# Moving small pieces of work in a fused adaLN, attention and expert-routing kernel

## The reference

```
mod = silu(c) @ wmod            # 4 x 6 x 512: sa, ca, ga, sb, cb, gb
ga, gb = sign(.) * max(abs(.), 0.25)
h = layernorm(x) * (1 + ca) + sa
q, k, v = h @ Wq + bq, h @ Wk + bk, h @ Wv + bv     # 16 heads of 128
a = softmax(q @ k.T / sqrt(128) + causal mask) @ v
x = x + ga * (a @ Wo + bo)
h = layernorm(x) * (1 + cb) + sb
w, idx = top2(softmax(h @ gate.T))                   # of 8 experts; w normalised to sum 1
y = sum over the 2 experts of w * (silu(h @ Wg.T) * (h @ Wu.T)) @ Wd.T
y = y + the same with the shared expert's weights    # 704 wide, no routing weight
return x + gb * y
```

## Time and profile before

| | |
|---|---|
| median of 3 runs (lowest to highest) | 1568.44 us (1567.68 to 1570.82) |
| the profiled execution / its span | 1572.1 us / 1569.9 us |
| mean granted TensorE clock | 0.989 of full speed |
| TensorE busy | 1520.4 us, 97% |
| VectorE busy | 1006.4 us, 64% |
| ScalarE busy | 731.9 us, 47% |
| GpSimd busy | 713.6 us, 45% |
| moved by DMA | 304.03 MB, mean 194 GB/s |

### The profile page before, as it was taken

How to read it: one execution, slowest core, us unless ns; L and a number is a source line. 1 busy time by engine, 2 the same in 40 slices (tenths; PEclk the granted TensorE clock), 3 DMA queues, 4 the chain that set the end, 5 groups by cost and what they waited for, 6 DMA issues and landing times.

```text
span 1569.9 us, 29503 instructions
## 1 busy us (share of the span) xinstructions
PE 1520.4 (97%) x8844; PEld 1355.2 (86%) x8844; DVE 1006.4 (64%) x2224; ACT 731.9 (47%) x1738; POOL 713.6 (45%) x761
## 2 busy tenths in 40 slices
PE   6899999998999999999999999998999999999998
PEld 3677778887999999999999999988989899999986
DVE  5876676667777777777777777795467322222268
ACT  2542222345666666666666666653331233333333
POOL 2103333346656566656565666667813211111055
PEclk9999999999999999999999999999999999999999
DMA  7334555568757666666757484653333456756455
GB/s 259 134 121 171 199 189 196 204 238 295 236 166 239 188 202 185 213 198 190 214 165 238 147 246 143 224 208 135 123 124 141 168 195 213 285 200 236 147 181 188
DMA packets 203292, 304.03 MB, mean 194 GB/s; under 512 B 80384, under 2 KB 142208, under 8 KB 196048
## 3 DMA queue, kind: packets, MB, share of 16 engines
q1 hardware_dynamic: 196096, 281.80, 53.1%
q0 software_dynamic: 5680, 18.62, 3.9%
q10 hardware_dynamic: 1440, 2.62, 0.5%
HBM read 187.35 MB, written 115.64 MB: 193 GB/s over the span
## 4 chain that ended last, share of the span: by engine, by line
PE 86%; DVE 6%; ACT 2%; issue 2%; DMA 2%; POOL 2%; another core or an unknown queue 0%; POOLq 0%; SPq 0%; ACTq 0%; DVEq 0%
PE bank L1553 45%; PE bank L1648 17%; PE bank L1763 8%; PE bank L1715 7%; PE bank L1746 4%; PE bank L1813 2%; PE bank L1566 1%; PE bank L1849 1%; DMA xin<-ffn_rows 1%; POOL h L1226 1%; ACT prob L1373 1%; DVE h_lo L2027 0%; POOL acc L1218 0%; ACT h_raw L1248 0%; DVE row_max L2200 0%
## 5 line engine op out<-in xcount | busy, mean ns | idle before, releaser
L1553 PE MATMUL bank<-w,xt_hi 128*128 (+2 forms) x1136 | 286.7, 334 | 10.8 <-DVE xt_lo L2176 7.8
L1553 PEld LDWEIGHTS bank<-w,xt_hi 128*128 128x128 f32 x1136 | 200.8, 192 | 17.8 <-issue 8.5
L1553 PE MATMUL bank<-w,xt_lo 128*128 (+2 forms) x568 | 186.1, 328 | 0.0
L1385 ACT ACTIVATE prob<-prob,row_inv 128x128 f32<-128x128 f32 (+3 forms) x256 | 137.2, 560 | 81.9 <-DVE row_inv L2213 81.9
L2349 DVE TENSOR_TENSOR ht_lo<-bank,ht_hi 128x128 fp32r<-128x128 f32 (+1 forms) x213 | 48.4, 282 | 185.0 <-ACT ht_hi L1493 181.2
L1373 ACT ACTIVATE prob<-bank,neg_max 128x128 f32<-128x128 f32 (+3 forms) x256 | 133.6, 525 | 44.0 <-DVE neg_max L2205 44.0
L1553 PE MATMUL bank<-wv_hi,h_hi 128*128 128x256 f32 x512 | 147.0, 287 | 0.0
L1553 PE MATMUL bank<-w,ht_hi 128*128 (+3 forms) x426 | 139.2, 408 | 6.5 <-DVE ht_lo L2349 5.7
L1553 PE MATMUL bank<-wv_hi,h_lo 128*128 128x256 f32 x512 | 144.7, 283 | 0.0
L1553 PE MATMUL bank<-wv_lo,h_hi 128*128 128x256 f32 x512 | 144.7, 283 | 0.0
L2200 DVE TENSOR_REDUCE row_max<-bank 128x1 f32<-128x128 f32 (+3 forms) x256 | 119.8, 489 | 6.6
(11 more groups left out here) (245 smaller groups left out, 4151.6 us busy)
## 6 DMA issues: line engine op xcount, KB each, us to landing
keys<-k_ring SPq DMA_DIRECT2D x64, 512.0 KB, 3.0
ch_raw<-wexp SPq DMA_DIRECT2D x128, 170.0 KB, 3.1
experts_hi<-ch_hi SPq DMA_DIRECT2D x128, 170.0 KB, 2.6
experts_lo<-ch_lo SPq DMA_DIRECT2D x128, 170.0 KB, 2.7
w<-experts_hi SPq DMA_DIRECT2D x10, 2176.0 KB, 7.9
w<-experts_lo SPq DMA_DIRECT2D x10, 2176.0 KB, 14.6
q_transposed<-q_out SPq DMA_DIRECT2D x64, 256.0 KB, 2.0
k_even<-keys SPq DMA_DIRECT2D x16, 1024.0 KB, 5.8
```

Of the source, the lines that this page charges most:

```text
L1385: ins = act.activation(part, part, ACT.Copy, scale=row_inv[:, h, r:r + 1])
L1553: ins = pe.matmul(dst, a, m, start=(k == 0), stop=(k == last))
```

## The change

1. **Modulation pieces.** Piece 1 goes to bank 0, so it no longer waits for the copy of piece 0. Pieces 3 and 2 are made right after the transposes of the first batch, into banks 6 and 7. Their weights go to a new buffer, `mod_early`, which lies where `t_parts0` lies later; SyncE issues their loads before the second batch's activations and no longer waits for the transposes. ScalarE copies piece 2 aside to `mod_raw`, and VectorE clamps it where it did. TensorE no longer makes piece 3 after plain(0) nor piece 2 after half 4.
2. **First attention step.** ScalarE and VectorE split the first group of values at the step's start, and the first transposed part before the last two normalisations.
3. **Norm rows of the first batch.** All four tiles are ScalarE's (one pass) and GpSimd's (two), in the last step. VectorE's `c_rows` is gone. GpSimd's passes stand between its residual passes for the second and third batch. The second batch's statistics are taken before the last additions to `acc` for two tiles and after the first split of stage 3 for the others; the split gate weights (`gate_columns`) come earlier.
4. **Slot tables.** Their three parts run one job sooner, the first two right after the gate product, and the third before the pass that adds up the shared result.
5. **Loops.** ScalarE's and VectorE's routed jobs are written out, 39 jobs, in place of the loop of two.

The two engines' order in the first attention step is in the diff. Cut to its core:

```diff
+        mod_early = sbuf(s1m, "mod_early", [P, 2, DC, D])
+        mod_raw = sbuf(s1, "mod_raw", [B, D])[:, :]
...
             sp.dma_start(stage[2], wq_v[:, :, 0:D]).then_inc(wq0_ld, 16)
+            mod_weights(3, mod_early[:, 0])
+            mod_weights(2, mod_early[:, 1])
             sp.dma_start(xs[1], x_t[:, TT:2 * TT, :]).then_inc(x_ld[0], 16)
             sp.wait_ge(mod_full, 1)
             raw_weights(0)
-            sp.wait_ge(tx_full, TT)
-            mod_weights(3, w_x)
...
-                if tail >= 0:
-                    loaded(tail)
-                    c_pre(tail)
-                if last:
+                if tail == 0:
+                    loaded(0)
+                    c_pre(0)
+                if tail == 1:
+                    loaded(1)
+                    c_pre(1, [0])
+                    c_rows(0, 0)
+                    c_pre(1, range(1, TT))
+                if tail == 2:
+                    c_rows(0, 1)
+                    loaded(2)
+                    c_pre(2, [0])
+                    c_rows(0, 2)
+                    c_rows(0, 3)
+                    c_pre(2, [1])
                     c_seed_of(1)
+                    c_pre(2, range(2, TT))
...
-                        act.wait_ge(mod_full, 3)
+                        act.wait_ge(mod_full, 4)
+                        act.activation(mod_raw, bank[7][0:B, :], ACT.Copy)
...
                 if first:
+                    v_part(0)
...
                     normalise(3, n)
-                    v_part(0)
                     exps(5, n)
+                    pt_part(0, 0)
                     normalise(4, n)
                     normalise(5, n)
-                    for g in range(3):
-                        pt_part(0, g)
+                    pt_part(0, 1)
+                    pt_part(0, 2)
...
                     v_part(0)
+                    if last:
+                        c_rows(0, 0)
...
                     normalise(5, n)
+                    if last:
+                        c_rows(0, 1)
...
+                else:
+                    c_rows(0, 2)
+                    c_rows(0, 3)
...
-            with act.Fori(R0 // 2 + 1, Z0 // 2 - 1) as j:
-                for k in range(2):
-                    job(j * 2 + k, k, "routed", True)
+            for n in range(R0 + 2, Z0 - 3):
+                job(n, n % 2, "routed", True)
...
-            mod_piece(1, stage[1], 6)
+            mod_piece(1, stage[1], 0)
...
             for i in range(1, TT):
                 transposes(0, i)
+            mod_piece(3, mod_early[:, 0], 6)
+            mod_piece(2, mod_early[:, 1], 7)
...
-                if b == 0:
-                    mod_piece(3, w_x, 6)
...
-                if norm2:
-                    c_rstd(0)
-                    c_rows(0, 0)
-                if norm3:
-                    gate_columns()
-                    c_rows(0, 2)
-                    c_rows(0, 3)
...
+            c_stats(1, 0)
+            c_stats(1, 1)
             for i in range(TT):
                 add_out(NIT - 1, B - 1, i)
-                c_stats(1, i)
+            xt_part(1, 1)
+            c_stats(1, 2)
+            c_stats(1, 3)
             c_moments(1)
-            xt_part(1, 1)
...
-                begun()
+                table()
...
-            shared_job(NT + 3, lambda: one_hots(1))
-            shared_job(NT + 4, tokens)
-            halves()
-            shared_job(NT + 5, table)
+            shared_job(NT + 3, lambda: one_hots(1), begun)
+            shared_job(NT + 4, tokens, halves)
+            shared_job(NT + 5)
...
-            with dve.Fori(R0 // 2 + 1, Z0 // 2) as j:
-                for k in range(2):
-                    job(j * 2 + k, k, "routed", True)
-            job(Z0 - 1, 0, "routed", True)
+            for n in range(R0 + 2, Z0):
+                job(n, n % 2, "routed", True)
```

More of the change, by code:

```diff
@@ L282, in adaln_layer @@
         s1 = ExitStack()
+        s1m = ExitStack()
+        mod_early = sbuf(s1m, "mod_early", [P, 2, DC, D])
+        s1m.close()
         t_both = [sbuf(s1, "t_parts0", [P, 12, T], F32R)]
@@ L426, in adaln_layer @@
         c_ld = sem("c_ld")
-        modw_ld = [sem("modw_ld0"), sem("modw_ld1"), sem("modw_ld_later")]
+        modw_ld = {0: sem("modw_ld0"), 1: sem("modw_ld1"), 3: sem("modw_ld_later"), 2: sem("modw_ld2")}
+        modw_ld[4] = modw_ld[5] = modw_ld[3]
         wq0_ld = sem("wq0_ld")
@@ L509, in adaln_layer @@
         c_seed = sem("c_seed")
-        c_xn = sem("c_xn")
         c_scaled = sem("c_scaled_rows")
@@ L619, in mod_weights @@
             def mod_weights(m, to):
-                sp.dma_start(to, wmod_v[:, :, m * D:(m + 1) * D]).then_inc(modw_ld[min(MOD_ORDER.index(m), 2)], 16)
+                sp.dma_start(to, wmod_v[:, :, m * D:(m + 1) * D]).then_inc(modw_ld[m], 16)
             def raw_weights(i):
@@ L1026, in c_rows @@
             def c_rows(b, t):
-                row, n = h2[:, t, :], (b - 1) * TT + t + 1
+                row, n = h2[:, t, :], b * TT + t + 1
                 pool.wait_ge(c_xa, n)
@@ L1035, in c_seed_of @@
                 pool.wait_ge(c_var, b + 1)
-                if b > 1:
-                    pool.wait_ge(c_xa, (b - 1) * TT)
+                if b:
+                    pool.wait_ge(c_xa, b * TT)
                 pool.tensor_tensor(rs0[:, :], ve[:, :], mh[:, :], ALU.pow).then_inc(c_seed, 1)
@@ L1237, in _ @@
                 act.wait_ge(mod_full, m + 1)
-                act.activation(mod_row[m], bank[6][0:B, :], ACT.Copy).then_inc(mod_ev, 1)
+                act.activation(mod_row[m], bank[(6, 0)[m]][0:B, :], ACT.Copy).then_inc(mod_ev, 1)
             def hidden(b, i):
@@ L1459, in c_rows @@
                 act.wait_ge(c_seed, (b + 1) * C_SEED)
-                act.wait_ge(h2_st, h2_stored(b - 1))
+                if b:
+                    act.wait_ge(h2_st, h2_stored(b - 1))
                 act.activation(h2[:, t, :], acc[:, b * TT + t, :], ACT.Identity, scale=rstd[:, t:t + 1],
@@ L1557, in _ @@
             pe.wait_ge(silu_c, 1)
+            MOD_FREE = {3: (mod_ev, 1), 2: (modc_ok, 2), 4: (mod_ev, 4), 5: (mod_ev, 5)}
             def mod_piece(m, w, to):
-                k = MOD_ORDER.index(m)
-                pe.wait_ge(modw_ld[min(k, 2)], 16 * max(k - 1, 1))
-                if k:
-                    pe.wait_ge(mod_ev, k)
+                pe.wait_ge(modw_ld[m], {4: 32, 5: 48}.get(m, 16))
+                if m in MOD_FREE:
+                    pe.wait_ge(*MOD_FREE[m])
                 for c in range(DC):
@@ L1624, in half @@
                                     [(q_ev, 11), (q_ev, 12), None, None, (q_ev, 13), (q_ev, 14), (q_ev, 15), (q_ev, 16)][m])
-                if v - 1 in MOD_AFTER:
+                if v - 1 in MOD_AFTER and MOD_AFTER[v - 1] != 2:
                     free[5] = (mod_ev, MOD_ORDER.index(MOD_AFTER[v - 1]) + 1)
@@ L1673, in half @@
                 product(6, plain_w(2, 1), t_rows(4))
-                if v in MOD_AFTER:
+                if v in MOD_AFTER and MOD_AFTER[v] != 2:
                     pe.wait_ge(*reader(v, 4))
@@ L2146, in half @@
                 if v in MOD_AFTER:
-                    mod_piece(MOD_AFTER[v], bank[half_banks(v + 1)[5]][0:B, :])
+                    m = MOD_AFTER[v]
+                    mod_piece(m, mod_raw if m == 2 else bank[half_banks(v + 1)[5]][0:B, :])
                 if v == 0:
@@ L2234, in step @@
                 norm2 = isinstance(p, int) and p == HP - 1 and b == 2
-                norm3 = isinstance(p, int) and p == HP - 1 and b == 3
                 if first:
+                    v_part(0)
                     maxima(0, n)
@@ L2288, in step @@
                     maxima(1, n + 1)
+                else:
+                    gate_columns()
                 o_part(1)
@@ L2320, in c_moments @@
                 dve.tensor_scalar(ve[:, :], mv[:, :, 1], EPS, None, ALU.add).then_inc(c_var, 1)
-            def c_rstd(b):
-                dve.wait_ge(c_seed, b * C_SEED + C_SEED)
-            def c_rows(b, t):
-                dve.scalar_tensor_tensor(out=h2[:, t, :], in0=acc[:, b * TT + t, :], scalar=mv[:, t, 0:1],
-                                         in1=mods[:, b, 2, :], op0=ALU.subtract, op1=ALU.mult).then_inc(c_xn, 1)
-                dve.wait_ge(c_xn, b * TT + (t + 1))
-                dve.scalar_tensor_tensor(out=h2[:, t, :], in0=h2[:, t, :], scalar=rstd[:, t:t + 1],
-                                         in1=mods[:, b, 1, :], op0=ALU.mult, op1=ALU.add).then_inc(h2_ok, 1)
             def gate_columns():
@@ L2362, in y_part, with job @@
                                   gb_row(b), ALU.mult).then_inc(y_gb, 1)
-            def job(n, s, prev, nxt, b_prev=None, after_xt=None):
+            def job(n, s, prev, nxt, b_prev=None, after_xt=None, after_mid=None):
                 if prev:
@@ L2371, in job @@
                 dve.tensor_tensor(h_mid[:, s, :], gate_s[:, s, :], bank[1][:, 0:F], ALU.mult).then_inc(mid_ok, 1)
+                if after_mid:
+                    after_mid()
                 if nxt:
```

(5 more changed lines are left out.)

4 lines of the change are left out of this document (removed).

## The result

| | before | changed |
|---|---|---|
| median (lowest to highest) | 1569.63 us (1567.68 to 1574.15), 4 runs | 1554.82 us (1553.15 to 1556.46), 4 runs |
| ratio, 95% interval | | 0.9899 (0.9876 to 0.9921) |
| span of the profiled execution | 1569.9 us | 1553.5 us |
| mean granted clock | 0.989 | 0.993 |

A forecast was written before the change was run, and what follows sets the result against it. TensorE, busy 97% of the span, was taken as the bound. Terms 1.75 + 3.60 + 0.4 + 4.15 + 4.1 + 5.0 = 19.0 us took the median from 1568.44 to 1549.4 us; 8-in-10 range 1544.5 to 1556.5 us.

The forecast's parts named there:

- First pause, +1.75 us: Before the first query products: pieces 3 and 2 keep TensorE working, saving 2.65 us, less 0.9 us at the second batch.
- The upper bound of 2.65 us: Top of the 0.95 to 2.65 us range for the net gain from filling the pause before the first query products.
- The give-back at the second batch: Without piece 3, idle there grows from 0.58 to about 4.2 us and the clock probably falls: 0.3 to 1.7, taken 0.9.
- Piece 2, +3.6 us: This modulation product leaves the stretch where TensorE never rests, saving 3.60 us.
- First attention step, +0.4 us: Splitting values 0 and 1 ahead of the score chain ends the second group of transposes about 0.4 us sooner (0 to 1.3).
- Norm rows, +4.15 us: Last attention steps to second shared job: VectorE freed, last weights then release TensorE; 3.35 us of wait plus 0.8 of clock.
- the wait's term: Before the second shared job: TensorE released by the last weights at 1061.5 us, not at 1064.85 us, gaining 3.35 us.
- the third rival: The clock survives the shortened waits at second batch (0.9 us), weights (1.7 us) and attention (1 us): 1545.8 us, chance 0.08.
- Slot tables, +4.1 us: First routed job: earlier tables remove 3.02 us of wait and 1.6 us of clock, less 0.5 us for TensorE's table read.
- Written-out loops, +5.0 us: Near the end: straight code cures two late "remote" instructions; TensorE gains 3.01 + 3.0 us, the end 5.0 (3.5 to 6).
- the first rival: Late instructions near the end are not the loops' doing but fall into GpSimd's first eight gathers and stay: 1554.4 us, chance 0.22.
- a range of its own: The forecast's span from its terms' ends, 1545.5 to 1553.5 us, carrying chance 0.53.

The follow-up runs named there:

- the second profile: Profile of the changed kernel run once more, without edits, on another chip than the four runs before it: 1550.42 us, ratio 0.9902 to the kernel before.
- the break: Changed kernel with GpSimd waiting after four of its first eight gathers until ScalarE has weighted two tiles: 1556.85 us, ratio 0.9929 to the kernel before.
- the best kernel: Changed kernel with a shorter wait amid the first eight gathers, all final additions on VectorE, modulation piece 3 after plain(0): 1546.41 us, ratio 0.9882 to before.
- the gathers spaced: Changed kernel with GpSimd waiting after its first four gathers until ScalarE has weighted two tiles: 1556.85 us, ratio 0.9929 to the kernel before.
- the tables back: Changed kernel with the slot tables' three parts at their old places: 1557.74 us, ratio 0.9937 to the kernel before.

## Why the prediction was right, and where not

- **First pause, +1.75 us.** Measured from the table: 2.4 and 2.5 us (3.36 - 0.92 and 3.30 - 0.77), 0.7 above the sum. The upper bound of 2.65 us does not follow from the terms: with 0.3 us given back at least it is 2.35, and the result lies just above that. The clock's 2.65 us came as 2.6 in every run with the change. The query products started 0.6 us sooner than the first piece's lead explains, where the sum had 0.05. The give-back at the second batch, 0.9 us, came as 0.74 and 0.66 us by 89.00 in the changed kernel and as 0.0 to 0.9 in its variants. The idle of 4.2 us there was 4.10, with the low clock behind it in every run. What the sum did not see: with one piece in the pause the query products run at full speed too, and the other piece behind plain(0) then gives 0.9 to 1.0 us.
- **Piece 2, +3.6 us.** 3.6 us in each run.
- **First attention step, +0.4 us.** 0.54 to 0.89, and 0.0 with the order undone. The sum has no term for the clock here. The two profiles with 0.9 us have a mean clock of 0.83 in the 10 us from the long wait's end, and a third with 0.54 has 0.67.
- **Norm rows, +4.15 us.** 3.6 and 3.7 us in the changed kernel. The last third of the weights released TensorE, as forecast. On the old axis (8.0 us later, the lead at 386.59) it landed at 1062.4 us against my 1061.5, the store ahead of it was issued at 1046.1 against 1045.8. So the wait's term was too large: 2.35 us in the first profile (lead 8.00 to 10.35), where the sum had 3.35. The clock's was too small in that profile: 2.2 us (10.35 to 12.59 six us further on) for 0.8. A tile's late load took 1.0 back. In the second profile it was 3.1 and 0.7. So the third rival, that the clock survives the shorter waits, came true at this place in two profiles of eleven and at the second batch in none.
- **Slot tables, +4.1 us.** 4.9 to 5.1. GpSimd's memset was no later than TensorE at all; I had kept back 0.5 us for a read that cost nothing, and 2 us come on top of the wait of 3.02 us, not 1.6.
- **Written-out loops, +5.0 us: failed.** The step "I take them for code that is not there yet, and straight code as the cure" is wrong. Straight code left both rows where they were. The words that I set against it (a stall stands at the branch, these stand jobs behind the loops' ends) were right, and the first rival, with 1554.4 us, was the outcome (1554.82). The DMA part of the trace says so too. Between 1482 and 1489 us, while both engines were late, no instruction queue moved anything; the last reads of these queues before lie between 1470 and 1482 us (the second block), and the second profile, without lateness, has the same two there:

```profile
q0 software_dynamic: 443, 1.43, 74.2%
q10 hardware_dynamic: 2, 0.00, 0.1%
```

```profile
q8 instruction: 1, 0.02, 0.5%
q14 instruction: 1, 0.01, 0.2%
```

The sum of what the second profile shows, 2.5 + 3.6 + 0.9 + 3.7 + 4.9 + 0 = 15.6 us, is near the ratio's 15.9.

So the measured time is right by the width of the range and by the first rival in it. The forecast itself had a range of its own, 1545.5 to 1553.5 us, and missed it: 5.0 us of its 19.0 were wrong in kind. That the miss is only 5.4 us has some luck in it. The other five terms came out 1.6 us above their sum of 14.0, with errors both ways. The range of its own isn't the sum of the terms' ends either; that sum is 1543.3 to 1557.1 us.

**What the lateness is.** In fourteen profiles the remote rows stand in five: the first of before and of the changed kernel, and three of the four runs on one chip, each with eight gathers in a row; TensorE's wait there is 1.4 to 3.0 us. The fourth on that chip had the break and none. On two other chips none of eight had them, five of these with the burst unbroken. So the burst alone is not enough: between 1482 and 1489 us the gathers keep the DMA engines busy for 68.0% in the second profile, with no lateness, and for 74.2% in the first. Something that differs between chips or executions must come to it. That the burst is needed, and the break the cure, rests on one profile. What delays a signal that TensorE has given by then to two engines at once is not settled.

## What to carry to other kernels

Ask of each late instruction without a releaser whether a second profile on another chip has it, before a cause is sought in the code; here it was a quarter of the forecast gain. Before work is moved into a pause, see which pause it fills now: piece 3 gave nothing in the first pause and left one of 4.10 us behind it. Read what a part gave from the lead across its own stretch, and look in several profiles whether the clock behind a wait falls each time, before a price is put on it. Before a transfer is moved ahead in a queue, see which store now waits behind it: the load that depends on that store sets the price.

## What was not expected of the hardware

A wait of 2.38 us before the second shared job was followed by a mean clock of 1.00 over 5.50 us, and one of 2.52 us before the same job by 0.69, in two executions of one kernel. In the first pause a wait of 2.12 us for modulation weights was followed by 1.00, and one of 2.06 us before the same piece, in the best kernel, by 0.63 over 4.67 us. The same piece of a program can thus lose its clock in one execution and keep it in another, and the length of the wait alone does not tell which: one job earlier, with the gathers spaced, a wait of 1.74 us was followed by 0.66 over 5.00 us. Longer waits gave one price: after the 3.02 us the mean over 5.00 us is 0.67 in the kernel before and 0.66 with the tables back. A transfer of 256 KB behind 1.4 MB of weights in the same queue took 6.9 us to be waited out, where 2.9 us were enough without them.
